# The last two token groups of a routed FFN: logits ahead of gate and up, rank between their halves, slot steps woven with the expert choice

## The chip, the cores and the metric

The kernel runs on one core of a Trainium2 chip. The metric is the device time of one execution in microseconds, lower is better. Engines as the profile names them: PE is TensorE, DVE is VectorE, ACT is ScalarE, POOL is GpSimd, SP is SyncE.

## The reference

One transformer layer on 4096 tokens (16 sequences of 256) of width 128, in float32. The first half is linear attention (16 heads of 8, prefix sums of k times v), with a layernorm before and after and a residual. The second half is a mixture of 16 experts with the top one chosen, beside a shared expert:

```python
logits = x @ w_router.T
_, top_idx = jax.lax.top_k(logits, TOP_K)
mask = jax.nn.one_hot(top_idx, E, dtype=logits.dtype).sum(axis=1)
scores = jax.nn.sigmoid(logits) * mask
masked_inputs = scores.T[:, :, None] * x[None, :, :]
gate_up = jnp.einsum('eth,ehf->etf', masked_inputs, gate_up_proj)
gate, up = jnp.split(gate_up, 2, axis=-1)
expert_out = jnp.einsum('etf,efh->eth', up * jax.nn.silu(gate), down_proj)
shared = jax.nn.silu(x @ w_gate.T) * (x @ w_up.T) @ w_down.T
out = shared + expert_out.sum(axis=0)
```

with x the layernorm of the residual, H = 128 wide, and F = 256 hidden.

## The kernel before, in words

There are three stages, each a loop that every engine runs in its own order; semaphores tie the engines together, and nothing but the order in the source decides which instruction of an engine comes next.

Stage one (`step1`) is the attention, over 32 tiles of 128 tokens. Stage three (`step3`) is the experts: the tokens lie sorted by expert in DRAM (`sorted_rows`), in 47 tiles that each belong to one expert, and each is loaded, projected, multiplied and scattered to the output.

The change lies in stage two (`step2`), which runs over 8 groups of 4 tiles (`NG` = 8, `GT` = 4). For group s:

- **PE**: gate and up of the shared expert for hidden half 0 (`gate_up_of(0)`, L1146 and L1148), the router's logits (L1157), gate and up of half 1, the transposes of the next group's normed tokens (L1165), then the shared down projection (L1193, `w_d`, 8 products in 16 instructions), and the rank: small bf16 products of the choice with triangular and full matrices of ones (L1174 to L1179) that count, for every token, how many earlier ones chose the same expert. In the last two groups, 6 and 7, the rank stands ahead of the down projection, in groups 0 to 5 behind it. PE's down projection waits for both halves of h.
- **ACT**: silu of each gate half (L605), the copy of the transposes (L609), the norms' products for later groups, tanh for the score (L631), the copy of the shared output (L634, L639). Behind the last group it copies the expert's down weights, which PE centres (L1218), into place (L656).
- **DVE**: h = silu times up, per half (L887); the choice, five steps of which each waits for the one before (L891 top, L895, L899, L903, L905 chosen, in `h_and_choice_steps`); and the slots of the group before, 19 steps, which turn rank and running totals into the row of `sorted_rows` for every token (`slot_steps`, L844 to L877). The last of them writes `slot_i` (L877). Up to group 5, norm steps for later groups (`prepare_steps`) run between these. For groups 6 and 7 there are none, and the order is: all 19 slot steps of the group before, h 0, choice, h 1.
- **POOL**: the score and scale of the group (L502 to L508), then four indirect DMAs (L518), one for each tile, that scatter the rows to their slots. It waits for `slot_i` of the group and for the shared output.

The code of POOL in stage two, cut to its waits:

```python
pool.wait_ge(s_scale, 2 * g + 2)
pool.wait_ge(s_sh_out, g + 1)
pool.wait_ge(s_slot, g + 1)
...
for t in range(GT * g, GT * (g + 1)):
    ...
    nc.gpsimd.indirect_dma_start(
```

SP issues the first load of stage three when all 32 scatters have landed (`s_scattered`). PE runs one matmul at that point (L1231).

Of the kernel before, what the change touches and what calls it, by code (L numbers as in the profile page):

```python
# [24 lines left out]
ALU = mybir.AluOpType  # L25
# [3 lines left out]
P = 128  # L29
# [5 lines left out]
def live(index, count):  # L35

    return not isinstance(index, int) or 0 <= index < count


def at_least(eng, sem, count):  # L40

    if not isinstance(count, int) or count > 0:
        eng.wait_ge(sem, count)
# [114 lines left out]
ALLOC_STEPS = 17  # L158
# [9 lines left out]
def build(nc, x, w_att, b_qkv, bo, w_ffn, gate_up, down, out):  # L168
# [3 lines left out]
    E = w_ffn.shape[1] % D  # L172
# [6 lines left out]
    GT = 4  # L179
    NG = NT // GT  # L180
# [17 lines left out]
    with ExitStack() as ctx:  # L198
# [13 lines left out]
        before_bf = sb("before_bf", [P, P], BF16)  # L212
        ones_bf = sb("ones_bf", [P, P], BF16)
# [14 lines left out]
        w_r = w_all[:, 2 * F + FC * D:2 * F + FC * D + E]  # L228
# [44 lines left out]
        xmT = sb("xmT", [P, 2, GD])  # L273
        silu_g = sb("silu_g", [P, FC, GD])
        hT = sb("hT", [P, FC, GD])
# [3 lines left out]
        chosen = sb("chosen", [P, 2, GT, E], BF16)  # L279
# [92 lines left out]
        s_silu = sem("shared_silu")  # L372
# [325 lines left out]
        def _(dve):  # L698
# [177 lines left out]
                sr.wait()  # L876
                yield nc.vector.tensor_copy(slot_i[:, tiles(GT * g, GT)], slot[:]).then_inc(s_slot, 1)  # L877

            def h_and_choice_steps(s, u):


                logits = ps_r[:, 0:GT * E].rearrange("p (k e) -> p k e", e=E)

                def h(f):
                    dve.wait_ge(s_silu, 2 * s + 1 + f)
                    at_least(dve, s_sh, s)
                    return nc.vector.tensor_tensor(hT[:, f, :], silu_g[:, f, :], ps_u[f][:], ALU.mult).then_inc(s_h, 1)  # L887
                routed_first = s >= NG - 2
                yield h(0)
                dve.wait_ge(s_logit, s + 1)  # L890
                yield nc.vector.tensor_reduce(top[:, u, :], logits, AX, ALU.max).then_inc(s_top, 1)  # L891
                if not routed_first:
                    yield h(1)
                dve.wait_ge(s_top, s + 1)
                yield nc.vector.tensor_tensor(  # L895
                    is_top[:], logits, top[:, u, :].rearrange("p (k o) -> p k o", o=1).to_broadcast([P, GT, E]),
                    ALU.is_equal).then_inc(s_route, 1)
                dve.wait_ge(s_route, 3 * s + 1)
                yield nc.vector.tensor_tensor(  # L899
                    is_top[:], is_top[:], from_last[:].rearrange("p (o e) -> p o e", o=1).to_broadcast([P, GT, E]),  # L900
                    ALU.mult).then_inc(s_route, 1)
                dve.wait_ge(s_route, 3 * s + 2)
                yield nc.vector.tensor_reduce(first_top[:], is_top[:], AX, ALU.max).then_inc(s_route, 1)  # L903
                dve.wait_ge(s_route, 3 * s + 3)
                yield nc.vector.tensor_tensor(  # L905
                    chosen[:, u, :, :], is_top[:],
                    first_top[:].rearrange("p (k o) -> p k o", o=1).to_broadcast([P, GT, E]),
                    ALU.is_equal).then_inc(s_chosen, 1)
                if routed_first:
                    yield h(1)  # L910

            def prepare_steps(s, u):

# [56 lines left out]
            step1(NT - 2, 2, prepare_steps(-2, 0))  # L970
            step1(NT - 1, 3)
            step1(NT, 0)
            for g in range(-1, NG + 1):
                step2(g, g % 2)


            dve.wait_ge(s_slot, NG)
            dve.wait_ge(s_iota, 4)
# [87 lines left out]
        def _(pe):  # L1066
# [75 lines left out]
            def step2(s, u):  # L1142
                def gate_up_of(f):
                    if live(s, NG):
                        at_least(pe, s_h, 2 * s - 1 + f)
                        nc.tensor.matmul(ps_g[f][:], w_g[:, f * P:(f + 1) * P], xmT[:, u % 2, :],  # L1146
                                         start=True, stop=True)
                        nc.tensor.matmul(ps_u[f][:], w_u[:, f * P:(f + 1) * P], xmT[:, u % 2, :],  # L1148
                                         start=True, stop=True).then_inc(s_gu, 1)

                if live(s, NG):
                    pe.wait_ge(s_xmT, s + 1)
                gate_up_of(0)
                if live(s, NG):
                    at_least(pe, s_chosen, s)
                    for k in range(GT):
                        ins = nc.tensor.matmul(ps_r[:, k * E:(k + 1) * E], xmT[:, u % 2, k * P:(k + 1) * P],  # L1157
                                               w_r, start=True, stop=True)
                    ins.then_inc(s_logit, 1)
                gate_up_of(1)  # L1160
                if live(s + 1, NG):
                    pe.wait_ge(s_xm, s + 2)
                    at_least(pe, s_xmT, s + 1)
                    for k in range(GT):
                        ins = nc.tensor.transpose(ps_t2[:, k * P:(k + 1) * P],  # L1165
                                                  xm[:, (u + 1) % 2, k * D:(k + 1) * D], ident[:])
                    ins.then_inc(s_xm_t, 1)
                def rank():


                    n = GT * E
                    pick = chosen[:, u, :, :].rearrange("p k e -> p (k e)")
                    pe.wait_ge(s_chosen, s + 1)
                    nc.tensor.matmul(ps_rank[:, 0:n], before_bf[:], pick, start=True, stop=False)  # L1174
                    for k in range(1, GT):
                        nc.tensor.matmul(ps_rank[:, k * E:n], ones_bf[:], pick[:, 0:n - k * E],
                                         start=False, stop=k == GT - 1)
                    for k in range(GT):
                        ins = nc.tensor.matmul(ps_rank[:, n:n + E], ones_bf[:], pick[:, k * E:(k + 1) * E],  # L1179
                                               start=k == 0, stop=k == GT - 1)  # L1180
                    ins.then_inc(s_rank, 1)
                if s >= NG - 2:
                    rank()
                if live(s, NG):
                    pe.wait_ge(s_h, 2 * s + 2)
                    at_least(pe, s_sh_out, s)
                    for k in range(GT):
                        for f in range(FC):
                            if s < NG - 1:
                                into = ps_y2[:, k * D:(k + 1) * D]  # L1190
                            else:
                                into = ps_last[k // 2][:, (k % 2) * D:(k % 2 + 1) * D]
                            ins = nc.tensor.matmul(into, hT[:, f, k * P:(k + 1) * P], w_d[:, f, :],  # L1193
                                                   start=f == 0, stop=f == FC - 1)
                        if k == GT - 1 or (s == NG - 1 and k == 1):
                            ins.then_inc(s_sh, 1)
                if live(s, NG) and s < NG - 2:
                    rank()
# [100 lines left out]
```

## Time and profile before

| | us |
|---|---|
| median of 3 runs | 329.99 (329.72 to 330.27) |
| profiled execution | 331.52 |
| its span | 329.70 |
| PE busy in the span | 271.9 (82%) |
| DVE busy | 278.7 (85%) |
| ACT busy | 191.8 (58%) |
| POOL busy | 189.7 (58%) |
| mean granted clock of PE | 0.929 of full speed |

Times in the trace are microseconds from the start of the span. A row of a timeline gives start, duration, engine, line of the kernel, operation, the tile written and those read, the shape, and how many instructions were merged; in brackets how long the engine was idle before it and what released it. An fp32 matmul shows as two records. Records of one engine can overlap, since a next instruction starts before the one before has ended. PEclk is the granted clock: 1.00 is 2.4 GHz, 0.50 is 1.2 GHz, and a value between is a stretch that holds both.

### The profile page before, as it was taken

The page shows a single profiled execution, that of the slowest core. Times are in us where ns is not written, and L with a number is a line of the kernel's source. Part 1 is how long each engine was busy: PE and PEld are TensorE (multiplying, and loading weights), DVE is VectorE, ACT ScalarE, POOL GpSimd, SP SyncE. Part 2 cuts the span into 40 slices and gives each one's busy share as a digit, 9 for nine tenths or more (in the row PEclk, how much of TensorE's full clock was granted, in tenths as well). Part 3 has the DMA queues.
Part 4 walks back from the last instruction along what each step waited for, and adds up shares of the span by engine and source line. Part 5 has one row for each costly group of instructions (what it writes and reads, how often), then busy time and mean ns, then how long its engine had stood idle before and what let it go on. Part 6 is the DMA issues. An engine that isn't in the chain of part 4 may idle for free.

```text
span 329.7 us, 6352 instructions
## 1 busy us (share of the span) xinstructions
PE 271.9 (82%) x1535; PEld 191.1 (58%) x1535; DVE 278.7 (85%) x1109; ACT 191.8 (58%) x581; POOL 189.7 (58%) x215
## 2 busy tenths in 40 slices
PE   3468999999999997746888888888599999999800
PEld 1224555556555553423455555558399999999800
DVE  5998999999999999998499998776039999999960
ACT  2325566566566563345566666434589999999400
POOL 5063876777776776300005555576102788888876
PEclk9977999999999999585699999999989999999975
DMA  6999920000000000000001111122599101111100
GB/s 172 368 431 378 421 99 0 2 3 0 0 2 2 0 2 0 0 1 3 0 0 66 67 66 65 67 83 81 155 338 305 32 22 36 40 43 35 33 28 0
DMA packets 13701, 28.41 MB, mean 86 GB/s; under 512 B 1982, under 2 KB 10182, under 8 KB 12642
## 3 DMA queue, kind: packets, MB, share of 16 engines
q1 hardware_dynamic: 10480, 21.57, 18.0%
q0 software_dynamic: 3040, 6.37, 5.7%
q8 instruction: 14, 0.23, 0.3%
q14 instruction: 21, 0.17, 0.2%
q10 hardware_dynamic: 146, 0.07, 0.1%
HBM read 15.38 MB, written 13.60 MB: 88 GB/s over the span
## 4 chain that ended last, share of the span: by engine, by line
DVE 42%; PE 42%; issue 6%; DMA 4%; POOL 3%; ACT 2%; ACTq 0%; SPq 0%; POOLq 0%; DVEq 0%
PE banks L1098 14%; PE banks L1117 6%; DVE hT_e L1031 5%; PE banks L1193 4%; DVE rows L1038 3%; DVE hT L887 3%; DVE rows L1002 3%; PE banks L1126 3%; PE banks L1146 2%; POOL out L536 2%; PE banks L1148 2%; DVE stats L1053 2%; DMA rows<-in_x 2%; PE banks L1086 2%; DVE stats L708 2%
## 5 line engine op out<-in xcount | busy, mean ns | idle before, releaser
L1098 PE MATMUL banks<-kv,upto 128*128 128x512 f32 x128 | 64.2, 626 | 1.3 <-POOL kv L491 1.3
L491 POOL TENSOR_TENSOR kv<-qk,vv 128x1024 f32<-128x1024 f32 x32 | 62.4, 1951 | 2.5
L536 POOL DMA_INDIRECT out<-rows,token_i x47 | 46.8, 997 | 10.5 <-issue 6.2
L1246 PE MATMUL banks<-xsT,w_now 128*128 128x128 f32 x376 | 52.2, 283 | 0.4 <-DVE hT_e L1031 0.3
L485 POOL TENSOR_TENSOR qk<-ex,rl 128x256 f32<-128x256 f32 x32 | 23.3, 728 | 46.0 <-ACT ex L592 46.0
L1246 PEld LDWEIGHTS banks<-xsT,w_now 128*128 128x128 f32 x376 | 46.9, 196 | 1.3 <-issue 1.1
L518 POOL DMA_INDIRECT sorted_rows<-rows,slot_i x32 | 31.7, 991 | 25.5 <-DVE slot_i L877 17.4
L791 DVE TENSOR_TENSOR prod<-banks,qk 128x1024 f32<-128x1024 f32 x32 | 39.0, 1218 | 1.9 <-PE banks L1098 1.3
L813 DVE TENSOR_REDUCE num<-prod 128x128 f32<-128x1024 f32 x32 | 38.6, 1207 | 0.0
L1098 PEld LDWEIGHTS banks<-kv,upto 128*128 128x128 f32 x128 | 23.3, 201 | 18.5 <-issue 17.0
L1031 DVE TENSOR_TENSOR hT_e<-silu_e,banks 128x256 f32<-128x256 f32 x47 | 19.3, 411 | 16.4 <-ACT silu_e L690 13.9
L1117 PE MATMUL banks<-w_qkvo,xnT 128*128 128x384 f32 x64 | 28.4, 528 | 5.2 <-DVE carry L782 2.9
L1254 PE MATMUL banks<-w_exp_down,hT_e 128*128 x188 | 28.8, 276 | 0.9 <-DVE rows L1038 0.9
L528 POOL TENSOR_TENSOR rows<-rows 128x128 f32<-128x128 f32 x34 | 16.1, 474 | 22.5 <-DVE rows L1002 22.0
L694 ACT COPY w_now<-w_exp 128x512 f32 x47 | 28.7, 610 | 0.0
L574 ACT COPY xnT<-banks 128x128 f32<-128x128 f32 x32 | 8.5, 265 | 34.0 <-PE banks L1105 20.1
L1254 PEld LDWEIGHTS banks<-w_exp_down,hT_e 128*128 128x128 f32 x188 | 24.8, 192 | 1.3 <-issue 1.3
L682 ACT ACTIVATE xs<-rows 128x128 f32<-128x128 f32 x47 | 23.2, 494 | 3.1 <-SPq L460 2.8
L1193 PE MATMUL banks<-w_d,hT 128*128 128x128 f32 x128 | 16.4, 281 | 9.3 <-DVE hT L887 9.3
L567 ACT ACTIVATE xn<-rows,nm,rs 128x128 f32<-128x128 f32 x32 | 16.4, 517 | 10.2 <-DVE nm L122 10.2
L690 ACT ACTIVATE silu_e<-banks 128x256 f32<-128x256 f32 x47 | 18.1, 385 | 6.0 <-PE banks L1246 4.8
L1193 PEld LDWEIGHTS banks<-w_d,hT 128*128 128x128 f32 x128 | 14.9, 191 | 10.9 <-DVE hT L887 10.9
(179 smaller groups left out, 653.3 us busy)
## 6 DMA issues: line engine op xcount, KB each, us to landing
sorted_rows<-rows SPq DMA_DIRECT2D x3, 1950.0 KB, 13.3
rows<-sorted_rows SPq DMA_DIRECT2D x10, 520.0 KB, 6.4
w_exp<-in_gate_up SPq DMA_DIRECT2D x4, 1024.0 KB, 20.2
w_exp_out<-in_down SPq DMA_DIRECT2D x4, 512.0 KB, 20.4
rows<-in_x SPq DMA_DIRECT2D x1, 1024.0 KB, 11.3
rows<-in_x SPq DMA_DIRECT2D x1, 768.0 KB, 8.5
out<-rows,token_i POOLq DMA_INDIRECT x47
sorted_rows<-rows,slot_i POOLq DMA_INDIRECT x32, 2.6
```

What stands on the lines that cost most here:

```text
L491: nc.gpsimd.tensor_tensor(kv[:, u, :].rearrange("p (h m d) -> p h m d", h=NH, m=HD), k, v, ALU.mult).then_inc(s_kv, 1)
L518: nc.gpsimd.indirect_dma_start(out=sorted_rows, out_offset=bass.IndirectOffsetOnAxis(ap=slot_i[:, t:t + 1], axis=0), in_=rows[:, t, :], in ...
L536: nc.gpsimd.indirect_dma_start(out=out_rows, out_offset=bass.IndirectOffsetOnAxis(ap=token_i[:, j - 1:j], axis=0), in_=rows[:, j - 1, 0:D] ...
L694: nc.scalar.copy(w_now[:, u % 2, :], flat(w_exp[:, bass.ds(e, 1), :])).then_inc(s_wn, 1)
L791: nc.vector.tensor_tensor(prod[:].rearrange("p (h m d) -> p h m d", h=NH, m=HD), ps_s[u % 2][:].rearrange("p (h m d) -> p h m d", h=NH, m=HD),
L813: nc.vector.tensor_reduce(num[:], prod[:].rearrange("p (n d) -> p n d", d=HD), AX, ALU.add).then_inc(s_chain, 1)
L1031: nc.vector.tensor_tensor(hT_e[:, u % 2, :], silu_e[:, u % 2, :], ps_gue[u % 2][:, F:2 * F], ALU.mult).then_inc(s_he, 1)
L1098: ins = nc.tensor.matmul(ps_s[u % 2][:, cols], upto[:], kv[:, u, cols], start=True, stop=True)
L1117: nc.tensor.matmul(ps_qkv[u % 2][:, 0:3 * D], xnT[:, u % 2, :], w_qkv, start=True, stop=True).then_inc(s_qkv, 1)
L1193: ins = nc.tensor.matmul(into, hT[:, f, k * P:(k + 1) * P], w_d[:, f, :], start=f == 0, stop=f == FC - 1)
L1246: ins = nc.tensor.matmul(ps_gue[u % 2][:, c * P:(c + 1) * P], w_now[:, u % 2, c * P:(c + 1) * P], xsT[:, u % 2, :], start=True, stop=True)
L1254: ins = nc.tensor.matmul(ps_ye[u % 2][:, 0:D], hT_e[:, u % 2, c * P:(c + 1) * P], flat(w_exp_down[:, bass.ds(e, 1), c, :]), start=c == 0, ...
```

## The change

In groups 6 and 7, and nowhere else:

- PE issues the logits ahead of gate and up of half 0, and the rank between the two halves instead of ahead of the down projection. `rank()` gets one more wait: that the first six slot steps of the group before, which read the bank that it writes, are done.
- DVE's order is written out in a loop of its own: six slot steps of the group before, then choice and slot steps in turn, h 0, the rest of the slot steps, eight slot steps of this group, h 1. The rest of this group's slot steps follow in the next round or at the end.

```diff
@@ DVE @@
-            def h_and_choice_steps(s, u):
-
+            def h(s, f):
+                dve.wait_ge(s_silu, 2 * s + 1 + f)
+                at_least(dve, s_sh, s)
+                return nc.vector.tensor_tensor(hT[:, f, :], silu_g[:, f, :], ps_u[f][:], ALU.mult).then_inc(s_h, 1)
+
+            def choice_steps(s, u):
...
-                routed_first = s >= NG - 2
-                yield h(0)
                 dve.wait_ge(s_logit, s + 1)
                 yield nc.vector.tensor_reduce(top[:, u, :], logits, AX, ALU.max).then_inc(s_top, 1)
-                if not routed_first:
-                    yield h(1)
...
-                if routed_first:
-                    yield h(1)
+
+            def h_and_choice_steps(s, u):
+
+                yield h(s, 0)
+                for n, ins in enumerate(choice_steps(s, u)):
+                    yield ins
+                    if n == 0:
+                        yield h(s, 1)
...
-            for g in range(-1, NG + 1):
+            for g in range(-1, NG - 2):
                 step2(g, g % 2)
 
+
+            def some(steps, count):
+                for _ in range(count):
+                    next(steps, None)
+
+            slots = slot_steps(NG - 3, (NG - 3) % 2)
+            for g in range(NG - 2, NG):
+                some(slots, 6)
+                for ins in choice_steps(g, g % 2):
+                    some(slots, 1)
+                h(g, 0)
+                some(slots, 99)
+                slots = slot_steps(g, g % 2)
+                some(slots, 8)
+                h(g, 1)
+            some(slots, 99)
@@ PE @@
+                def logits():
+                    if live(s, NG):
+                        at_least(pe, s_chosen, s)
+                        for k in range(GT):
+                            ins = nc.tensor.matmul(ps_r[:, k * E:(k + 1) * E], xmT[:, u % 2, k * P:(k + 1) * P],
+                                                   w_r, start=True, stop=True)
+                        ins.then_inc(s_logit, 1)
+
+                def rank():
...
+                    pe.wait_ge(s_chosen, s + 1)
+                    at_least(pe, s_alloc, ALLOC_STEPS * (s - 1) + 6)
...
                 if live(s, NG):
                     pe.wait_ge(s_xmT, s + 1)
...
+                if s >= NG - 2:
+                    logits()
+                    gate_up_of(0)
+                    rank()
+                else:
+                    gate_up_of(0)
+                    logits()
                 gate_up_of(1)
...
-                if s >= NG - 2:
-                    rank()
```

PE, group 6, in the kernel before (banks2 and banks4 are half 0's and half 1's gate and up, banks0 logits, banks6 transposes and rank; the last row is the down projection):

```order
L1146 MATMUL banks2<-xmT,w_ffn 128x512
L1148 MATMUL banks4<-xmT,w_ffn 128x512
L1157 MATMUL banks0<-w_ffn,xmT 128x16 x4
L1146 MATMUL banks2<-xmT,w_ffn 128x512
L1148 MATMUL banks4<-xmT,w_ffn 128x512
L1165 MATMUL banks6<-ident,xm 128x128 x4
L1174 MATMUL banks6<-chosen,before_bf 128x64
L1176 MATMUL banks6<-chosen,ones_bf 128x48
L1176 MATMUL banks6<-chosen,ones_bf 128x32
...
L1179 MATMUL banks6<-chosen,ones_bf 128x16 x4
L1193 MATMUL banks0<-w_d,hT 128x128 x8
```

The same stretch of PE with the change:

```order
L1172 MATMUL banks0<-w_ffn,xmT 128x16 x4
L1163 MATMUL banks2<-xmT,w_ffn 128x512
L1165 MATMUL banks4<-xmT,w_ffn 128x512
L1183 MATMUL banks6<-chosen,before_bf 128x64
...
L1188 MATMUL banks6<-chosen,ones_bf 128x16 x4
L1163 MATMUL banks2<-xmT,w_ffn 128x512
L1165 MATMUL banks4<-xmT,w_ffn 128x512
L1206 MATMUL banks6<-ident,xm 128x128 x4
L1218 MATMUL banks0<-w_d,hT 128x128 x8
```

The logits moved from behind gate and up of half 0 to ahead of them, the rank from behind the transposes to between the halves, and the down projection keeps its place behind the transposes.

DVE, group 6 before, from the last slot steps of group 5 (`slot_i`) to the first of group 6:

```order
L875 TENSOR_REDUCE slot<-slot_of 128x4
L877 CAST slot_i<-slot 128x4
L887 TENSOR_TENSOR hT<-silu_g,banks 128x512
L891 TENSOR_REDUCE top<-banks 128x4
L895 TENSOR_TENSOR is_top<-banks,top 128x64
L899 TENSOR_TENSOR is_top<-is_top,from_last 128x64
L903 TENSOR_REDUCE first_top<-is_top 128x4
L905 TENSOR_TENSOR chosen<-is_top,first_top 128x64
L887 TENSOR_TENSOR hT<-silu_g,banks 128x512
L844 TENSOR_TENSOR taken<-taken,banks 128x16
```

DVE with the change, from the last steps of the choice of group 6 on (all `L853` to `L877` rows up to `slot_i` are of group 5):

```order
L898 TENSOR_REDUCE first_top<-is_top 128x4
L859 TENSOR_SCALAR all_ends<-given,all_ends 128x16
L900 TENSOR_TENSOR chosen<-is_top,first_top 128x64
L862 TENSOR_TENSOR shift_new<-all_ends,room 128x16
L882 TENSOR_TENSOR hT<-silu_g,banks 128x512
L864 TENSOR_TENSOR shift_gain<-shift_new,shift 128x16
...
L875 TENSOR_REDUCE slot<-slot_of 128x4
L877 CAST slot_i<-slot 128x4
L844 TENSOR_TENSOR taken<-taken,banks 128x16
```

And the rows that follow, up to h 1 of group 6 (`L845` to `L855` are of group 6):

```order
L851 TENSOR_TENSOR slot_of<-banks,shift_taken 128x64
L853 TENSOR_SCALAR need<-need 128x16
L855 SCALAR_TENSOR_TENSOR given<-ones,need 128x16
L882 TENSOR_TENSOR hT<-silu_g,banks 128x512
L856 TENSOR_TENSOR room<-room,need 128x16
```

h 0 came behind `slot_i` of group 5 and stands ahead of it now, with slot steps 12 to 19 of group 5 (L864 to L877) behind it; h 1 came ahead of group 6's first slot step and stands behind eight of them.

## Rows read from the trace of the kernel before

**Rows 1.** The chain that ended last, shares of the span by engine (page).

```profile
DVE 42%; PE 42%; issue 6%; DMA 4%; POOL 3%; ACT 2%; ACTq 0%; SPq 0%; POOLq 0%; DVEq 0%
```

**Rows 2.** The chain around the last scatter: start us, us, what.

```profile
231.27 3.27 DMA sorted_rows<-rows,slot_i
...
234.56 1.96 DMA rows<-sorted_rows
```

**Rows 3.** Timeline of POOL, scatters that open groups 5, 6 and 7.

```profile
214.12 1.03 POOL L518 DMA_INDIRECT sorted_rows<-rows,slot_i  x1 [0.36 <-POOL rows L508]
...
220.00 1.03 POOL L518 DMA_INDIRECT sorted_rows<-rows,slot_i  x1 [0.37 <-POOL rows L508]
...
227.40 1.03 POOL L518 DMA_INDIRECT sorted_rows<-rows,slot_i  x1 [1.85 <-DVE slot_i L877]
```

**Rows 4.** Timeline of DVE, groups 5 to 7, slot steps, choice and h.

```profile
211.47 0.17 DVE L864 TENSOR_TENSOR shift_gain<-shift_new,shift 128x16 f32<-128x16 f32 x1
...
212.80 0.25 DVE L877 CAST slot_i<-slot 128x4 int32<-128x4 f32 x1
...
213.48 0.22 DVE L891 TENSOR_REDUCE top<-banks 128x4 f32<-128x64 f32 x1
...
214.50 0.23 DVE L905 TENSOR_TENSOR chosen<-is_top,first_top 128x64 bf16<-128x64 f32 x1
214.70 0.69 DVE L887 TENSOR_TENSOR hT<-silu_g,banks 128x512 f32<-128x512 f32 x1
215.30 0.16 DVE L844 TENSOR_TENSOR taken<-taken,banks 128x16 f32<-128x16 f32 x1
...
216.53 0.15 DVE L856 TENSOR_TENSOR room<-room,need 128x16 f32<-128x16 f32 x1
...
224.25 0.20 DVE L856 TENSOR_TENSOR room<-room,need 128x16 f32<-128x16 f32 x1
...
226.38 0.17 DVE L877 CAST slot_i<-slot 128x4 int32<-128x4 f32 x1
```

**Rows 5.** Timeline of PE, rank of group 5 to down projection of group 7.

```profile
209.25 0.19 PE L1174 MATMUL banks<-chosen,before_bf 128*128 128x64 bf16 x1
...
209.46 1.10 PE L1146 MATMUL banks<-xmT,w_ffn 128*128 128x512 f32 x2
...
211.26 0.96 PE L1157 MATMUL banks<-w_ffn,xmT 128*128 128x16 f32 x8
212.07 1.10 PE L1146 MATMUL banks<-xmT,w_ffn 128*128 128x512 f32 x2
...
213.87 0.60 PE L1165 MATMUL banks<-ident,xm 128*128 128x128 f32 x4
...
215.44 2.05 PE L1193 MATMUL banks<-w_d,hT 128*128 128x128 f32 x16 [0.29 <-DVE hT L887]
217.33 1.02 PE L1146 MATMUL banks<-xmT,w_ffn 128*128 128x512 f32 x2
...
223.23 2.05 PE L1193 MATMUL banks<-w_d,hT 128*128 128x128 f32 x16 [1.08 <-DVE hT L887]
```

**Rows 6.** Timeline of ACT: silu 1 of group 6, last copy of the centring.

```profile
214.07 0.60 ACT L605 ACTIVATE silu_g<-banks 128x512 f32<-128x512 f32 x1 [2.01 <-PE banks L1148]
...
233.22 0.59 ACT L656 COPY w_exp_down<-banks 128x512 f32<-128x512 f32 x1 [0.31 <-PE banks L1218]
```

**Rows 7.** Timeline of PE, holes in stage two and at the end of stage one.

```profile
134.17 1.62 PE L1117 MATMUL banks<-w_qkvo,xnT 128*128 128x384 f32 x2 [2.29 <-DVE zq L777]
...
207.36 2.05 PE L1193 MATMUL banks<-w_d,hT 128*128 128x128 f32 x16 [1.63 <-DVE hT L887]
```

**Rows 8.** Stretches: us, busy by engine, PEclk, DMA share, GB/s.

```profile
132.00:133.00 1.00, 0.00 (x0) 0.00 (x0) 0.93 (x5) 0.18 (x1) 0.00 (x0) 0.73 0.00 0
...
238.00:239.00 1.00, 0.33 (x2) 0.33 (x3) 0.00 (x0) 0.88 (x2) 0.00 (x0) 0.63 1.07 346
...
241.00:242.00 1.00, 1.00 (x8) 1.00 (x7) 0.42 (x1) 1.00 (x3) 0.00 (x0) 0.66 1.04 358
```

More of the change, by code:

```diff
@@ L877, in slot_steps @@
                 yield nc.vector.tensor_copy(slot_i[:, tiles(GT * g, GT)], slot[:]).then_inc(s_slot, 1)
-            def h_and_choice_steps(s, u):
-                logits = ps_r[:, 0:GT * E].rearrange("p (k e) -> p k e", e=E)
[L884 to L887, printed above, removed]
-                routed_first = s >= NG - 2
-                yield h(0)
+            def h(s, f):
[3 more added lines that the diff above has]
+            def choice_steps(s, u):
+                logits = ps_r[:, 0:GT * E].rearrange("p (k e) -> p k e", e=E)
                 dve.wait_ge(s_logit, s + 1)
                 yield nc.vector.tensor_reduce(top[:, u, :], logits, AX, ALU.max).then_inc(s_top, 1)
-                if not routed_first:
-                    yield h(1)
                 dve.wait_ge(s_top, s + 1)
@@ L1149, in gate_up_of @@
                                          start=True, stop=True).then_inc(s_gu, 1)
+                def logits():
[6 more added lines that the diff above has]
+                def rank():
+                    n = GT * E
+                    pick = chosen[:, u, :, :].rearrange("p k e -> p (k e)")
+                    pe.wait_ge(s_chosen, s + 1)
+                    at_least(pe, s_alloc, ALLOC_STEPS * (s - 1) + 6)
+                    nc.tensor.matmul(ps_rank[:, 0:n], before_bf[:], pick, start=True, stop=False)
+                    for k in range(1, GT):
+                        nc.tensor.matmul(ps_rank[:, k * E:n], ones_bf[:], pick[:, 0:n - k * E],
+                                         start=False, stop=k == GT - 1)
+                    for k in range(GT):
+                        ins = nc.tensor.matmul(ps_rank[:, n:n + E], ones_bf[:], pick[:, k * E:(k + 1) * E],
+                                               start=k == 0, stop=k == GT - 1)
+                    ins.then_inc(s_rank, 1)
                 if live(s, NG):
                     pe.wait_ge(s_xmT, s + 1)
[L1153 to L1159, printed above, removed]
+                if s >= NG - 2:
[5 more added lines that the diff above has]
+                    logits()
                 gate_up_of(1)
@@ L1167, in step2 @@
                     ins.then_inc(s_xm_t, 1)
[L1168 to L1181, printed above, removed]
-                if s >= NG - 2:
-                    rank()
                 if live(s, NG):
```

## The prediction

> **What bounds the kernel now.** I read the chain of waits first, by engine: DVE 42% and PE 42%, POOL 3% [rows 1]. The average says nothing of this change, which touches only token groups 6 and 7, the last two of the second stage. There the question is what the last scatter waits for, because the third stage loads nothing until all 32 scatters have landed [rows 2]. So I read POOL's timeline next. One group's scatters and score steps fill POOL for 5.88 us: group 5 starts scattering at 214.12, group 6 at 220.00, each with only 0.36 to 0.37 us of idle before it, behind POOL's own L508 [rows 3]. POOL is therefore the bound from 214.12 on. Of these three groups only group 7 waits for VectorE: 1.85 us before 227.40 [rows 3], for the slot_i of 226.38 [rows 4]. Taking off the 0.37 that a start has anyway, POOL loses 1.48 us to VectorE there. That is all that an earlier slot_i of group 7 can bring, unless group 5 also started earlier, which POOL forbids. The reader should keep two numbers: from the start of a slot_i record to the first scatter 1.02 us (226.38 to 227.40 [rows 3, 4]), and slack: group 5's slot_i starts at 212.80 [rows 4], so 213.82 would do where POOL starts at 214.12. It has 0.3 us of slack, no more.
>
> **Group 6, step by step.** No instruction is added or removed; one wait is added (the rank for six allocation steps of the group before), and it is met long before. On PE the logits now start at 209.46, where gate 0 started, and gate and up 0 follow 0.81 later (211.26 to 212.07 for the same logits [rows 5]), at 210.27. From a gate's start to its silu are 2.00 us (212.07 to 214.07 [rows 5, 6]), silu takes 0.60 and h starts 0.03 later [rows 4, 6]. So h 0 of group 6 can't start before 212.90.
>
> On VectorE the six first slot steps of group 5 start when the rank is counted, at about 209.6 (209.25 and some 0.3 [rows 5]), and take six eighths of the 1.23 below; they are done by 210.5, when the logits are there too (209.46 + 0.96 for their record [rows 5]). The woven choice: top to chosen is four spacings in 1.02 us, 0.26 each [rows 4], and a slot step fits into each, so chosen(6) is written by about 211.8, 2.9 us earlier than now (214.50 + 0.23). The rank on PE finds it ready. That much works as the change says.
>
> But then VectorE stands in front of h 0 until 212.90 with slot steps 12 to 19 of group 5 **queued behind it**. h holds the engine 0.60 (214.70 to 215.30), and from step 12 to slot_i are 1.33 (211.47 to 212.80) [rows 4]. slot_i of group 5 starts at 212.90 + 0.60 + 1.33 = 214.83 instead of 212.80, and its scatters at 215.85 instead of 214.12. The slack of 0.3 is gone and POOL is 1.73 late. With two more groups of 5.88 us, group 7 can't start before 215.85 + 11.76 = 227.61, against 227.40 now. The 1.48 that could be won is spent already.
>
> Next, eight slot steps of group 6 stand ahead of its h 1: they begin at 214.91 (about half a record after slot_i), take 1.23 (215.30 to 216.53 [rows 4]), so h 1 starts at 216.14, though its silu is ready at about 214.9 (gate 1 starts at 210.27 + 1.81 + 0.20 for the rank = 212.28 [rows 5]). h 1 is 0.69 long and w_d follows 0.05 later: 216.88, against 215.44 now [rows 4, 5]. PE meanwhile runs gate and up 1 (1.80), then the transposes, whose record ends 0.60 after their start at 214.09, at 214.69. **PE stands idle for 2.2 us, 214.69 to 216.88**, where it now has 0.29.
>
> **Group 7.** w_d takes 1.89 (215.44 to 217.33 [rows 5]), so the logits start at 218.77 and are there at 219.79. VectorE has finished step 14 of group 6 at about 217.9 and waits. Choice and steps 15 to 19 woven take five spacings: slot_i of group 6 starts near 221.0, its scatters at max(222.0, 215.85 + 5.88 = 221.73) = 222.0, and group 7 can't start before 227.9. On PE gate and up 0 start at 219.58, gate 1 at 221.59 after the rank, its silu ends 2.60 later, h 1 runs at 224.22 and w_d at 224.96 (now 223.23 [rows 5]). Steps 9 to 19 follow h 1: 224.82 + 2.13 (224.25 to 226.38 [rows 4]) = 226.95 for slot_i, 227.97 for the first scatter. Both limits agree: **227.95, 0.55 us later than now**, if PE keeps its clock. The expert weights' centring behind it on PE, and ScalarE's copies of it, move by 1.73 with w_d: their last copy ends at 235.5 instead of 233.81 [rows 6]. The load for which the third stage waits arrives at 236.5 now (234.56 + 1.96 [rows 2]) and later with the change, so the centring stays hidden; it would cost only from about 1.5 us more. The rest of the kernel moves as one piece.
>
> **The clock.** The hole of 2.2 us is new in this stretch. Now the longest hole here is 1.63 us [rows 7], and the granted clock stays at 1.00. The hole of 2.29 us ahead of 134.17 [rows 7] is the nearest row in length: the clock fell to its lower level (1.2 GHz) within it, at 0.73 mean in 132 to 133 [rows 8], though PE had run little just before it as well. The hole ahead of the third stage does the same: by the means 0.63 and 0.66 of two stretches it falls at about 238.3 and comes back at about 241.7 [rows 8], some 3.4 us at the lower level. So I price a fall by that row: 3.4 us at half speed is 1.7 us of PE's work lost. Its place is w_d of group 6 and the logits and gates of group 7, where PE has no idle until gate 1 and where both limits above hang on PE. Part of it may lie in the hole, so 1.5 to 1.7 reach the last scatter; I take 1.5. Lower bound 0 (the 1.63 row, no fall). Upper bound: a second such stretch, 3.4. I choose the fall, since 2.2 is nearer to 2.29 than to 1.63.
>
> The Trainium skill ("TensorE: Matmul & The Clock Gate", "What's actually happening") says that the activity monitor looks at stretches which do not begin with the kernel, so one and the same hole can cost in one execution and not in the next. By that rule the sum is 0.55 in some runs and 2.05 in others; the trace has one execution and can't show it, and the case without a fall is the first rival.
>
> A second rule speaks against the weave. In the rows, neighbours that don't depend on each other overlap: steps 1 to 8 take 1.23 us, 0.15 each, with records of 0.15 to 0.25 [rows 4], and the steps of the choice, each of which waits for the one before, are 0.26 apart. The Trainium skill ("VectorE: DVE Perf Modes", "The DRAIN you can't avoid") says that the next operation starts only when the pipe is empty and that waits cost nothing on top; by it weaving wins nothing. The rows disagree; it is a rival with a small chance below.
>
> **Sum.** 0.55 + 1.5 = 2.05 us later. The profiled execution took 331.52 for a span of 329.70, so it would be 333.6; its 1.8 us outside the span don't change. The runs shown have a median of 329.99, 1.5 below it, and there the forecast is **332.0**. A measurement can tell 0.2% from no change here, 0.66 us.
>
> **Rivals.**
> - *PE keeps its clock in the new hole.* For it: 2.2 lies between 1.63 and 2.29, and the latter had little work ahead of it. Then the last scatter is 0.55 late: 330.5. My start times carry perhaps 0.3 of error, so a third of this case is slower by over 0.66, the rest is the same. Chance 0.32.
> - *Not slower, but faster: POOL never waits.* If slot_i of group 5 were out by 213.1, scatters would keep 5.88 us and group 7 would start at 225.9: 1.48 earlier, 328.5. It decides at silu 0 of group 6: it would have to end by 211.2, or h 0 not stand ahead of the slot steps. The order says it does, and the logits alone push the gates to 210.27. Chance 0.07.
> - *The clock stays up ahead of the third stage*, as centring now ends later and shortens that hole. It wins at most 1.7 of PE's time, 1.1 after what ScalarE's copies then bound (an estimate from the same stretch, rows 8): 329.4, up to 1.15 below now. Chance 0.06, half of it faster.
> - *Weaving wins nothing.* Five pairs of 0.22 and 0.17 [rows 4] take 1.95 instead of 1.3 in group 7, so slot_i of group 6 and both scatters behind it move 0.65: 331.2. Chance 0.05.
>
> **How the numbers follow.** The forecast has 0.50. Faster: 0.07 + 0.03 = 0.10. The same: two thirds of 0.32 and 0.03, 0.25. Slower: 0.50 + 0.05 + a third of 0.32, 0.65 rounded. The range takes in the case without a fall with its error downward (329.99 + 0.55 - 0.5, rounded to 330.0) and upward the fall at 1.7 with the same error plus part of a second low stretch, 332.8. Left out are the faster cases and a full second stretch, under 0.2. Slower cases alone: 330.7 to 332.8.
>
> **What would show it.** Right: group 5's first scatter at 215.8 with idle before it put down to slot_i; slot_i of group 6 near 221; a PE hole of about 2.2 us before w_d of group 6; h 0 of group 6 waiting for silu; a granted clock below 1.00 between 217 and 222, and the last four scatters from 229.5 (from 228 without the fall). Wrong: group 5 scattering at 214.1, or w_d of group 6 before 216.

## The result and the profile after

| | before | changed |
|---|---|---|
| first comparison, median of 4 runs each | 330.13 (329.72 to 330.27) | 334.71 (333.59 to 335.35) |
| second comparison, 25 and 12 runs | 332.44 | 335.08 (331.49 to 337.08) |
| profiled execution, its span | 331.52, 329.70 | 333.59, 331.80 |

The changed kernel is slower: ratio 1.0102 [1.0059, 1.0144] in the first comparison and 1.0081 [1.0046, 1.0115] in the second. (The medians of the first row alone would give 1.0139.) The ratios leave out executions over 1.5% above the fastest of their kernel, among them five of 345 us and more in the later comparisons, while medians and ranges take in all. The kernel before turned out to vary more than its first runs showed; in the later comparisons its medians were 332.45, 332.44 and 331.69. So the absolute times of different comparisons aren't to be set against each other, and the traces are read by stretches. The stretch that isolates the change runs from group 4's first scatter, which the change doesn't touch, to group 7's first. It took 19.15 us before, from this row to the 227.40 of [rows 3]:

```profile
208.25 1.03 POOL L518 DMA_INDIRECT sorted_rows<-rows,slot_i  x1 [3.19 <-DVE slot_i L877]
```

The page's chain by engine is nearly that of [rows 1]; it tells nothing of the change. The line of granted clocks does: it has a dip to 5 in slice 27, where the page of before (first line) shows 9.

```profile
PEclk9977999999999999585699999999989999999975
```

```profile
PEclk9977999999999999775799999959979999999955
DVE 42%; PE 42%; issue 6%; DMA 3%; POOL 3%; ACT 2%; SPq 0%; ACTq 0%; POOLq 0%; DVEq 0%
```

POOL's timeline of the changed kernel, the first scatters of groups 4 to 7, answers to [rows 3]:

```profile
207.03 1.03 POOL L518 DMA_INDIRECT sorted_rows<-rows,slot_i  x1 [3.19 <-DVE slot_i L877]
...
214.68 1.03 POOL L518 DMA_INDIRECT sorted_rows<-rows,slot_i  x1 [2.13 <-DVE slot_i L877]
...
222.19 1.03 POOL L518 DMA_INDIRECT sorted_rows<-rows,slot_i  x1 [2.00 <-DVE slot_i L877]
...
229.99 1.03 POOL L518 DMA_INDIRECT sorted_rows<-rows,slot_i  x1 [2.29 <-ACT rows L639]
```

Groups 5 and 6 had 0.36 and 0.37 us of idle ahead of them and now have 2.13 and 2.00. The stretch is 22.96 us, 3.81 longer. The last wait is put down to ACT's copy, but slot_i is what it was: the next view has it at 228.97, and the scatter comes 1.02 later, the same lag as in the kernel before.

DVE's timeline, for [rows 4]; L882 is h, L888 the top, L900 the choice:

```profile
209.32 0.23 DVE L888 TENSOR_REDUCE top<-banks 128x4 f32<-128x64 f32 x1
209.46 0.17 DVE L853 TENSOR_SCALAR need<-need 128x16 int32<-128x16 int32 x1
209.58 0.23 DVE L890 TENSOR_TENSOR is_top<-banks,top 128x64 f32<-128x64 f32 x1
...
210.37 0.22 DVE L900 TENSOR_TENSOR chosen<-is_top,first_top 128x64 bf16<-128x64 f32 x1
...
211.77 0.69 DVE L882 TENSOR_TENSOR hT<-silu_g,banks 128x512 f32<-128x512 f32 x1 [0.98 <-ACT silu_g L605]
...
213.72 0.17 DVE L877 CAST slot_i<-slot 128x4 int32<-128x4 f32 x1
...
215.02 0.67 DVE L882 TENSOR_TENSOR hT<-silu_g,banks 128x512 f32<-128x512 f32 x1
...
220.03 0.22 DVE L888 TENSOR_REDUCE top<-banks 128x4 f32<-128x64 f32 x1 [3.22 <-PE banks L1172]
...
221.22 0.17 DVE L877 CAST slot_i<-slot 128x4 int32<-128x4 f32 x1
...
228.97 0.17 DVE L877 CAST slot_i<-slot 128x4 int32<-128x4 f32 x1
```

The weaving works: a slot step lies between top and is_top, which are 0.26 apart as they were without it, and the choice takes 1.05 us with its slot steps inside. Then h 0 waits 0.98 for silu with the rest of group 5's slot steps behind it. Group 5's first scatter comes 7.65 after group 4's, where it was 5.87.

PE's timeline, for [rows 5] (L1206 transposes, L1218 down projection, L1172 logits, L1163 gate), and the granted clock of three stretches, for [rows 8]:

```profile
212.94 0.60 PE L1206 MATMUL banks<-ident,xm 128*128 128x128 f32 x4
215.74 2.73 PE L1218 MATMUL banks<-w_d,hT 128*128 128x128 f32 x16 [2.20 <-DVE hT L882]
218.26 1.73 PE L1172 MATMUL banks<-w_ffn,xmT 128*128 128x16 f32 x8
219.83 2.05 PE L1163 MATMUL banks<-xmT,w_ffn 128*128 128x512 f32 x2
...
227.09 2.05 PE L1218 MATMUL banks<-w_d,hT 128*128 128x128 f32 x16 [1.41 <-DVE hT L882]
```

```profile
216.00:217.00 1.00, 1.00 (x11) 1.00 (x11) 0.71 (x5) 0.00 (x0) 0.96 (x1) 0.97 0.44 145
217.00:218.00 1.00, 1.00 (x7) 1.00 (x6) 0.00 (x0) 0.00 (x0) 0.72 (x1) 0.50 0.38 133
...
223.00:224.00 1.00, 1.00 (x10) 0.60 (x9) 0.00 (x0) 0.37 (x1) 0.69 (x2) 0.62 0.24 87
```

The hole ahead of the down projection is 2.20 us, and behind it the clock goes to 1.2 GHz, by the means 0.97 and 0.62 from 216.9 to 223.8: 6.8 us. The records of the logits (1.73) and of the gate (2.05) there are about twice as long as in [rows 5] (0.96 and 1.02 to 1.10). ACT's last copy of the centring (copying the centred expert weights into place), which was at 233.22 [rows 6], is not in the way: the third stage's first xs comes 1.0 us after its end.

```profile
236.83 0.59 ACT L656 COPY w_exp_down<-banks 128x512 f32<-128x512 f32 x1 [0.31 <-PE banks L1243]
...
238.42 0.49 ACT L682 ACTIVATE xs<-rows 128x128 f32<-128x128 f32 x1 [1.01 <-SPq L460]
```

### The profile page after: what moved, and what is told of

Its sections match the earlier page's. It is cut to its first block, busy times and chain, and to the rows that moved or that the text cites. A ratio compares the mean times of both kernels' runs of the same rounds, so it can differ in the third digit from the quotient of the medians.

```text
span 331.8 us, 6359 instructions
## 1 busy us (share of the span) xinstructions
PE 273.9 (83%) x1535; PEld 192.8 (58%) x1535; DVE 276.4 (83%) x1109; ACT 191.7 (58%) x581; POOL 189.8 (57%) x215
## 4 chain that ended last, share of the span: by engine, by line
DVE 42%; PE 42%; issue 6%; DMA 3%; POOL 3%; ACT 2%; SPq 0%; ACTq 0%; POOLq 0%; DVEq 0%
PE banks L1115 14%; PE banks L1134 5%; DVE hT_e L1048 5%; PE banks L1218 5%; DVE hT L882 3%; DVE rows L1055 3%; DVE rows L1019 3%; PE banks L1163 2%; PE banks L1143 2%; POOL out L536 2%; PE banks L1165 2%; DVE stats L1070 2%; DVE stats L708 2%; PE banks L1271 2%; DMA rows<-in_x 2%
## 5 line engine op out<-in xcount | busy, mean ns | idle before, releaser
L1218 PE MATMUL banks<-w_d,hT 128*128 128x128 f32 x128 | 17.1, 289 | 11.3 <-DVE hT L882 11.3
L1218 PEld LDWEIGHTS banks<-w_d,hT 128*128 128x128 f32 x128 | 15.5, 197 | 13.8 <-DVE hT L882 13.8
```

## The experiments

The theory has two parts: the order makes group 5's scatters late, and it opens a hole in which the clock falls. The rival: the order itself costs the time and the clock is a bystander. Each experiment is judged by the stretch from group 4's first scatter to group 7's, and by its timed runs beside the kernel before on the same chip. All stretches are collected behind the last of them.

**Filling the hole.** Three idle matmuls (their result is not used), then one, between group 6's transposes and its down projection, into columns of a bank that nobody else uses at that time:

```diff
                     ins.then_inc(s_xm_t, 1)
+                if s == NG - 2:
+                    for _ in range(3):
+                        nc.tensor.matmul(ps_r[:, P:4 * P], ident[:], w_g_u[:, 0:3 * P], start=True, stop=True)
```

> The changed kernel, with three idle 128x384 fp32 matmuls on PE in the hole ahead of group 6's down projection (some 2.1 us of work in a hole of 2.20). Theory (the change costs 0.55 us by the late scatters of group 5 and about 3.3 us by a fall of PE's clock that the hole brings on): the clock stays at 1.00 from 205 to 235, the slot order is as it was, the median is some 0.6 us above the kernel before, 330.7 (330.3 to 331.2). Rival (the clock is a bystander, the new order itself costs the time): 334 or more, as the changed kernel.

> The changed kernel with one such idle matmul, 0.7 us, so that a hole of some 1.5 us is left, a little shorter than the 1.63 us hole that the kernel before has in stage two. Theory: the clock stays up as it did there, the time is that of the kernel with three, 330.7. If what is left is still enough for a fall in some executions, the median lies between 331 and 334 and the runs spread. Rival: 334 or more.

With three the ratio was 1.0040 [1.0008, 1.0072], with one 0.9997 [0.9972, 1.0023]: some 1.3 us above the kernel before and level with it, where 0.6 above was expected of both. PE and POOL with three, and last PE with one:

```profile
215.81 2.10 PE L1211 MATMUL banks<-w_ffn,ident 128*128 128x384 f32 x6
218.16 2.05 PE L1221 MATMUL banks<-w_d,hT 128*128 128x128 f32 x16 [0.25 <-DVE hT L882]
```

```profile
209.47 1.03 POOL L518 DMA_INDIRECT sorted_rows<-rows,slot_i  x1 [3.19 <-DVE slot_i L877]
...
217.09 1.03 POOL L518 DMA_INDIRECT sorted_rows<-rows,slot_i  x1 [2.13 <-DVE slot_i L877]
...
229.33 1.03 POOL L518 DMA_INDIRECT sorted_rows<-rows,slot_i  x1 [0.64 <-ACT rows L639]
```

```profile
218.31 2.05 PE L1221 MATMUL banks<-w_d,hT 128*128 128x128 f32 x16 [1.53 <-DVE hT L882]
```

The hole is gone and the clock stays at 1.00 up to the third stage. The order is unaltered: group 5 is as late as before (2.13 of idle). The stretch is 19.86 us instead of 22.96, 0.71 over the kernel before, and exactly the same with one idle matmul, which leaves a hole of 1.53. So 3.10 us of the 3.81 hang on the clock and 0.71 on the order. In this stretch the two kernels do the same. What sets their ratios apart isn't shown. Both profiles, and that of the next experiment, have a low stretch of 6.8 us at the start of the third stage, where the kernel before and the changed kernel have one of 3.4, and 103.0 to 103.7 us from group 7's first scatter to the end instead of 101.5 to 102.4. Whether the order has a part in that was not tested.

**h 1 first.** In group 6, `h(g, 1)` ahead of `some(slots, 8)`.

> The changed kernel with h 1 of group 6 ahead of that group's eight slot steps; nothing else moves and PE gets no idle work. Theory: the down projection starts 1.2 us earlier, the hole shrinks from 2.20 to about 1.0 us, the clock stays up, and the last scatters start about 0.2 us later than in the kernel before (group 5's are still late): 330.4 (330.0 to 330.9). Rival (late slot steps are what costs): no gain over the changed kernel, 334 or more, since group 6's slot steps come later still.

```profile
214.95 2.05 PE L1222 MATMUL banks<-w_d,hT 128*128 128x128 f32 x16 [0.98 <-DVE hT L882]
```

The hole closes to 0.98 by one swap on DVE, without idle work. The clock stays up there, the stretch is 19.45 (0.30 over the kernel before, 0.2 was expected) and the ratio 1.0002 [0.9974, 1.0031]. Later slot steps of group 6 cost nothing; the rival falls here too.

**The changed kernel again.** It was timed in more executions, and profiled three times more.

> The changed kernel unaltered, timed in more rounds and beside the experiments. Theory: from group 4's first scatter to group 7's first are 23 us with one or two stretches at the lower clock after the hole of 2.2 us, against 19.15 before; a stretch of 3.4 us makes it about 21.5, two of them (6.8 us, as in the first profile) 23. The median is 2 to 4.5 us above the kernel before. Rival (the first comparison fell on a bad set of executions): within 1 us of the kernel before.

> The changed kernel again, for its profile alone: how long the stretch at the lower clock behind group 6's hole is in another execution. If one fall always costs two such stretches here, it is 6.8 us as in both profiles so far, and group 7's first scatter comes 23.0 us after group 4's. If it was chance, it is 3.4 us in some, and 21.5 us.

> As the look before it: 6.8 us and 23.0 us, or 3.4 us and 21.5 us.

The stretches were 23.04, 22.96 and 21.51 us, in the second, third and fourth profile of this kernel. POOL in the third, then in the fourth, groups 4 and 7, and the ends of the low stretch in the fourth:

```profile
208.76 1.03 POOL L518 DMA_INDIRECT sorted_rows<-rows,slot_i  x1 [3.19 <-DVE slot_i L877]
...
231.72 1.03 POOL L518 DMA_INDIRECT sorted_rows<-rows,slot_i  x1 [2.46 <-ACT rows L639]
```

```profile
207.86 1.03 POOL L518 DMA_INDIRECT sorted_rows<-rows,slot_i  x1 [3.19 <-DVE slot_i L877]
...
229.37 1.03 POOL L518 DMA_INDIRECT sorted_rows<-rows,slot_i  x1 [0.63 <-POOL rows L508]
```

```profile
217.00:217.50 0.50, 0.50 (x6) 0.50 (x5) 0.43 (x4) 0.00 (x0) 0.50 (x1) 0.72 0.80 274
...
220.50:221.00 0.50, 0.50 (x5) 0.50 (x6) 0.00 (x0) 0.00 (x0) 0.41 (x3) 0.87 0.27 100
```

The clock fell in all four profiles of this kernel, 0.7 to 1.4 us after the down projection began. In three it stayed low for some 6.8 us and in one for some 3.4 (217.2 to 220.6), with PE busy throughout. The price was 3.1 to 3.2 in the three and 1.65 in the one, each against 19.86. The whole times of these profiled executions, 333.59, 335.48, 335.07 and 333.55, don't sort by it: the first had the long stretch and the fourth the short one.

**All of group 5's slots first.** `some(slots, 99)` ahead of `h(g, 0)`, in both groups.

> The changed kernel with all of group 5's slot steps ahead of h 0 of group 6 (and group 6's ahead of h 0 of group 7). Theory: group 5's scatters start within 0.3 us of where POOL is ready, so the 1.7 us are not lost; h 1 of group 6 comes about 1 us earlier as VectorE doesn't idle ahead of h 0, the PE hole is about 1.2 us and the clock stays up; the last scatters start 0.4 us earlier than in the kernel before: 0.4 us faster (0 to 0.9). Rival (the waiting h 0 costs nothing): group 5's first scatter still has over 1.5 us of idle before it.

> The kernel with all of group 5's slot steps ahead of h 0 once more, since its first profile fell on an execution of over 550 us that tells nothing. Theory and rival as for the first: group 5's scatters within 0.3 us of POOL's own work, a PE hole of about 1.2 us, the clock up, the four last scatters 0.4 us earlier than in the kernel before, measured from group 4's first; the median, by the first set, at that of the kernel before within 0.3%.

The medians were 332.55 beside 332.44 (ratio 1.0009 [0.9979, 1.0040]) and 331.85 beside 331.69. Group 5's scatters start at POOL's own pace (idle 0.57), as the theory says. The hole ahead of the down projection is 1.43, and the clock stays up. But group 7's come at 19.15, just as in the kernel before: the expected 0.4 isn't there. Group 6 explains it, with an idle of its own:

```profile
215.16 1.03 POOL L518 DMA_INDIRECT sorted_rows<-rows,slot_i  x1 [0.57 <-POOL rows L508]
...
222.11 1.03 POOL L518 DMA_INDIRECT sorted_rows<-rows,slot_i  x1 [1.47 <-DVE slot_i L877]
```

Its last slot steps are woven with the choice of group 7, and so wait for logits that stand behind the down projection on PE.

**Each half alone.** DVE's order of the changed kernel with PE's of before, and the reverse.

> VectorE's new order alone, PE's order as before. Theory: the choice, now ahead of h 0, waits for logits that PE still gives only behind gate and up 0, 1.8 us later than in the changed kernel; slot_i of group 5 and its scatters come 2.4 us later than in the kernel before, the hole ahead of group 6's down projection is about 2.9 us and the clock falls: 3 to 6 us slower than the kernel before, no less than the changed kernel. Rival (the cost lies in PE's new order): near the kernel before.

> PE's new order alone, VectorE's as before. Theory: the rank stands between PE's halves and waits for a choice that VectorE still makes behind h 0, so PE idles 2.5 us ahead of the rank of group 6 and again in group 7; group 5's scatters keep their time, group 6's come 2 us later, group 7's 5 to 6 us later without any fall of the clock and more with one: 7 to 10 us slower than the kernel before. Rival (PE's order is harmless without VectorE's): within 1 us of the kernel before.

DVE's order alone: 335.41 beside 332.44, but its six times run from 329.67 to 338.02 and give no ratio, so the reading rests on the stretch, 23.54. PE's holes there:

```profile
218.92 3.38 PE L1215 MATMUL banks<-w_d,hT 128*128 128x128 f32 x16 [2.82 <-DVE hT L882]
...
229.19 3.40 PE L1215 MATMUL banks<-w_d,hT 128*128 128x128 f32 x16 [2.05 <-DVE hT L882]
```

The clock fell behind both, for about 3.4 us each. PE's order alone: ratio 1.0260 [1.0202, 1.0318], stretch 27.60. PE waits for the choice ahead of both ranks:

```profile
215.50 0.24 PE L1181 MATMUL banks<-chosen,before_bf 128*128 128x64 bf16 x1 [2.64 <-DVE chosen L900]
...
227.92 0.20 PE L1181 MATMUL banks<-chosen,before_bf 128*128 128x64 bf16 x1 [2.58 <-DVE chosen L900]
```

PE's came out at 8.9 by the medians, within the 7 to 10 us that the theory gave; group 6's scatters came 4.1 later where 2 were expected, and the clock fell here too, at 215.5 for 3.4 us and at 229.1 for 6.8. DVE's came out at 2.97, just under its 3 to 6. By the stretch, either half alone is slower than the kernel before.

**By what is due.** PE's order kept, DVE's written anew:

```diff
+            slots = slot_steps(NG - 3, (NG - 3) % 2)
+            some(slots, 6)
+            for ins in choice_steps(NG - 2, (NG - 2) % 2):
+                some(slots, 1)
+            some(slots, 99)
+            h(NG - 2, 0)
+            slots = slot_steps(NG - 2, (NG - 2) % 2)
+            some(slots, 6)
+            h(NG - 2, 1)
+            some(slots, 99)
+            for ins in choice_steps(NG - 1, (NG - 1) % 2):
+                pass
+            slots = slot_steps(NG - 1, (NG - 1) % 2)
+            some(slots, 2)
+            h(NG - 1, 0)
+            some(slots, 8)
+            h(NG - 1, 1)
+            some(slots, 99)
```

> PE's order of the changed kernel, VectorE's order written anew by what is due: all of group 5's slot steps before h 0 of group 6, h 1 of group 6 after six slot steps, group 6's slot steps done before the choice of group 7, h 1 of group 7 after ten or so of its slot steps. Theory: group 5's scatters start behind POOL's own work again, POOL has no gap of over 0.6 us in front of groups 5, 6 and 7, the PE hole is about 1 us and the clock stays up: the 1.3 to 1.48 us that POOL waits in the kernel before are won, 328.8 (328.4 to 329.3). Rival (the PE order with the logits first costs by itself): not below the kernel before, 330 or more.

```profile
208.75 1.03 POOL L518 DMA_INDIRECT sorted_rows<-rows,slot_i  x1 [3.19 <-DVE slot_i L877]
...
214.82 1.03 POOL L518 DMA_INDIRECT sorted_rows<-rows,slot_i  x1 [0.57 <-POOL rows L508]
...
220.73 1.03 POOL L518 DMA_INDIRECT sorted_rows<-rows,slot_i  x1 [0.37 <-POOL rows L508]
...
226.78 1.03 POOL L518 DMA_INDIRECT sorted_rows<-rows,slot_i  x1 [0.47 <-ACT rows L639]
```

POOL runs through: 18.03 us, 1.12 less than before, where 1.3 to 1.48 were expected. The median was 329.83 (328.50 to 331.29), ratio 0.9941 [0.9917, 0.9965]. With PE's new order a kernel faster than before is possible, once DVE serves group 5's scatters first. How much of it is PE's order isn't shown: no run has a DVE order by what is due with PE's order of before.

**The clock ahead of the third stage.** A second idle matmul behind the one that was there, and one behind the first transpose of stage three, in the kernel just shown, in the kernel before, and in the changed kernel with the hole filled:

```diff
+            for _ in range(2):
                 nc.tensor.matmul(ps_idle[:], ident[:], w_g_u[:, 0:4 * P], start=True, stop=True)
...
+                    if j == -3:
+                        nc.tensor.matmul(ps_idle[:], ident[:], w_g_u[:, 0:4 * P], start=True, stop=True)
```

> The kernel whose VectorE order goes by what is due, with two more idle 128x512 matmuls on PE ahead of the third stage: one behind the one that is there already, one behind the first transposes. Theory (a fall of the clock comes from holes, here the two of about 1.15 us and the one before them): the clock stays at 1.00 from 230 to 245 and the time is about 1 us less than without them, 3.5 us below the kernel before. Rival (these first tiles are bound by ScalarE and the loads): within 0.4 us of the kernel without them.

> The kernel before with the two idle matmuls ahead of the third stage. Theory: the clock stays at 1.00 from 230 to 245, the stretch from group 7's first scatter to the end is 1 us shorter, the median 1 to 1.5 us below the kernel before, and the runs spread less, since the length of that low stretch differs between executions. Rival: within 0.4 us of the kernel before.

> The changed kernel with both fillings, three idle matmuls in group 6's hole and two ahead of the third stage. Theory: no fall of the clock from 165 on, so what is left against the kernel before with the second filling is the late start of group 5's scatters and the shift of 0.71 us that the trace showed between group 4's first scatter and group 7's: 0.7 us above that kernel (0.3 to 1.1). Rival (the change costs something else than these two): 1.5 us or more above it.

The stretch 230 to 246 of the kernel before and then of the same with the two matmuls; the third figure from the end of the line is the granted clock:

```profile
230.00:246.00 16.00, 11.77 (x81) 10.37 (x80) 1.99 (x7) 10.38 (x26) 1.92 (x2) 0.89 0.74 235
```

```profile
230.00:246.00 16.00, 13.17 (x93) 10.58 (x92) 2.39 (x8) 11.05 (x27) 2.13 (x3) 1.00 0.71 227
```

The clock stays up in all three kernels. The kernel before with it gave 330.13 beside 331.69, ratio 0.9965 [0.9938, 0.9992], where 1 to 1.5 us less were expected; the kernel by what is due gave 329.38 beside 332.44, ratio 0.9915 [0.9880, 0.9949], 3.1 us less where 3.5 were expected. That the filling adds to the latter rests on the trace (group 7's first scatter to the end 100.53 instead of 101.62) more than on the ratios, whose intervals overlap. The changed kernel with both fillings had a median of 331.77, 1.6 above the kernel before with the second filling, which is the rival's case (1.5 or more); by their ratios, 0.9975 [0.9935, 1.0016] and 0.9965, the two are some 0.3 us apart. So time decides nothing here: the two spread over 6.1 and 2.5 us. The traces give 19.85 against 19.13 for the stretch, the expected 0.7, and behind it 101.03 against 101.39, no further cost.

| kernel | group 4's first scatter to group 5's | to 6's | to 7's | 7's to the end |
|---|---|---|---|---|
| before | 5.87 | 11.75 | 19.15 | 102.30 |
| changed | 7.65 | 15.16 | 22.96 | 101.81 |
| changed, second profile | 7.65 | 15.28 | 23.04 | 101.77 |
| changed, third profile | 7.63 | 15.00 | 22.96 | 101.48 |
| changed, fourth profile | 7.64 | 15.37 | 21.51 | 102.43 |
| hole filled, 3 | 7.62 | 13.73 | 19.86 | 102.97 |
| hole filled, 1 | 7.62 | 13.74 | 19.86 | 103.72 |
| h 1 first | 7.63 | 13.53 | 19.45 | 103.49 |
| slots first | 6.07 | 13.02 | 19.15 | 101.26 |
| DVE's order alone | 8.16 | 17.62 | 23.54 | 101.16 |
| PE's order alone | 5.88 | 15.87 | 27.60 | 103.21 |
| by what is due | 6.07 | 11.98 | 18.03 | 101.62 |
| the same, third stage filled | 6.07 | 11.98 | 18.03 | 100.53 |
| before, third stage filled | 5.87 | 11.75 | 19.13 | 101.39 |
| changed, both filled | 7.62 | 13.73 | 19.85 | 101.03 |

## Why the prediction was right in its mechanism and wrong in its size

The forecast was 332.0, range 330.0 to 332.8, with 0.65 for slower. Slower it was, by the mechanism that had 0.50, and outside the range.

- **POOL as the bound, group 5 late behind the waiting h 0:** right. 1.73 us were forecast; all runs with this order show 1.75 to 1.78 (7.62 to 7.65 against 5.87).
- **Group 7's last scatters without a fall of the clock:** 0.55 forecast, 0.71 measured in the two kernels with the hole filled.
- **The hole:** 2.2 us forecast, 2.20 measured, at the place named.
- **The clock falls behind it:** right, in four profiles of four. The rival in which PE keeps its clock had 0.32 and did not occur; with the hole of 1.53 the clock stayed up, with those of 2.18 to 2.20 it never did.
- **The price of the fall is the step that failed.** "I price a fall by that row: 3.4 us at half speed ... I take 1.5." That is what one profile of four shows (1.65). The other three have a low stretch of 6.8 us and a price of 3.1 to 3.2. The text named a second stretch, 3.4, as the upper bound and then left it out of the range; it was the common case. (Its "part of a second low stretch" is not in the number either: 329.99 + 0.55 + 1.7 + 0.5 is 332.74.) The trace of before had the long case, behind the very hole of 2.29 that the prediction chose as the nearest in length. By the 0.73 of 132 to 133 [rows 8] and the 0.72 below, the clock was low there from 132.5 to 139.3, 6.8 us, with PE busy from 135 on:

```profile
135.00:135.50 0.50, 0.50 (x2) 0.10 (x1) 0.50 (x3) 0.00 (x0) 0.00 (x0) 0.50 0.00 0
...
138.50:139.00 0.50, 0.50 (x2) 0.30 (x1) 0.50 (x4) 0.14 (x1) 0.50 (x1) 0.50 0.00 0
139.00:139.50 0.50, 0.50 (x2) 0.19 (x1) 0.50 (x2) 0.00 (x0) 0.50 (x1) 0.72 0.00 0
```

From 146.1 to 163.2 it was low for 17 us more. That the clock falls was taken from the one row and how long from another; one row was used as the length of a thing that has several lengths.
- **The starting point:** 329.99 was the low end of what the kernel before does. Beside a median of 332.4 the changed kernel is 2.6 us slower, beside 330.1 it is 4.6. The stretches say 3.8 for a long fall. How much of the rest is the draw of executions stays open. That the profiled execution took 333.59, as the prediction's 333.6 for such a one, is luck: its stretch is 3.81 longer and not 2.05, while group 4's first scatter came 1.22 earlier than in the profile of before and the part behind the stretch was 0.49 shorter.
- **The rival that weaving wins nothing:** wrong. A pair of records 0.23 and 0.17 us long starts 0.14 and 0.12 apart, so the next operation starts before the record ahead of it has ended. The section of the Trainium skill that the prediction cites for this rival ("VectorE: DVE Perf Modes", "The DRAIN you can't avoid") says so too in a sentence that the prediction left out: a next operation that is not held starts earlier. The trace agrees with that sentence.
- **That the clock stays up ahead of the third stage:** the centring did move, and the clock fell there all the same in the changed kernel (the profile has it low from 240.8 to 244.2).
- On the clock the Trainium skill ("TensorE: Matmul & The Clock Gate", "What's actually happening") says that the monitor's stretches run freely, so that one hole needn't cost the same twice. The runs agree in the length, 3.4 us low in one execution and 6.8 in three for the same instructions, but not in the case that the prediction drew from it: no execution profiled was without the fall.

What the runs leave open is why the stretch is short or long. In stage two the eight falls that were profiled sort by their start: the four that came 0.7 us or less behind the end of the idle time, or just ahead of it, lasted 3.4 us, and the four that came 1.0 to 1.4 behind it 6.8. But behind the 2.29 at the end of stage one it is the other way round: low from 132.5, inside the hole, for 6.8 us in the kernel before, and from 135.0, 1.25 behind its end, for 3.4 in the changed one. So this is no rule.

## What to carry to other kernels

When work moves ahead on one engine, list what is now queued behind each of its waits: here the choice came 2.9 us early and made no scatter earlier, because a product that waits for silu was put in front of slot steps that POOL was waiting for. Before reordering, work out the longest idle time that PE gets and compare it with holes in the trace after which the granted clock fell; if it comes near, close it by order or with idle matmuls. A fall should be priced by every low stretch that the trace shows behind a like hole, the nearest one first: here that one was 6.8 us long, and the price was taken from another of 3.4.

## What the runs showed of the hardware that was not expected

- A low stretch is not of one length. Seen in stage two and at the start of stage three: 3.4 or 6.8 us, four of each in stage two. At the end of stage one it was 17 us (13.7 in one profile), in the kernel before with PE busy all the time in its last 8 us.
- In stage two the clock fell at each hole of 2.05 to 2.82 us and at none of 1.64 us or less.
- The same program differs by about 4 us between executions: the kernel before ran from 329.9 to 333.7 in the 35 executions of one comparison. Part of it shows in the traces: group 4's first scatter, up to which these kernels don't differ, lay between 207.0 and 209.7 us, and the time from group 7's first scatter to the end between 101.2 and 103.7 without the filling.
- One swap on DVE (h 1 ahead of eight small steps) was worth at least as much as 2.1 us of idle matmuls on PE (a stretch of 19.45 against 19.86): the clock fell behind neither of the idle times that were left (0.98 and 0.25 us).
